# Attention on one core: 64-row products moved in among the scores, and a diagonal block between transposes

## What is computed

```python
xn = layernorm(inputs)                       # gamma, beta
q, k, v = xh @ Wq + bq, xh @ Wk + bk, xh @ Wv + bv     # per head
content = einsum('bqhd,bkhd->bhqk', q + u_bias, k)
pos_score = _rel_shift(einsum('bqhd,khd->bhqk', q + v_bias, p))
attn = softmax((content + pos_score) / sqrt(e))
ctx = einsum('bhqk,bkhd->bqhd', attn, v)
x = layernorm(x + ctx @ Wo + bo)
```

## Time and profile before

| | us |
|---|---|
| median of 3 runs (lowest, highest) | 553.13 (547.18, 553.98) |
| the profiled execution | 551.84 |
| its span, first to last instruction | 550.0 |
| TensorE busy | 452.6 |
| VectorE busy | 356.1 |
| ScalarE busy | 267.4 |
| GpSimd busy | 249.2 |

### The profile page before, as it was taken

The page is one execution under the profiler, slowest core; times in us unless marked ns, Lnnn a source line. Parts: engine busy times, 40 slices in busy tenths (PEclk is TensorE's granted clock), DMA queues, the critical chain, the costliest instruction groups (busy, mean ns, idle before and its releaser), DMA issues. The chain is left out here.

```text
span 550.0 us, 9872 instructions
## 1 busy us (share of the span) xinstructions
PE 452.6 (82%) x3109; PEld 317.3 (58%) x3109; DVE 356.1 (65%) x893; ACT 267.4 (49%) x547; POOL 249.2 (45%) x260
## 2 busy tenths in 40 slices
PE   8798999999999999999857799738979798428870
PEld 7565666656656566666434799613454466327760
DVE  4976676676876777667434466367486566638882
ACT  2356567666666565777401355517546222025653
POOL 3452563446572862440033154442445466425771
PEclk9999999999999999999886899958989978659995
DMA  8499999999999000000040230090000000013405
GB/s 308 109 174 172 170 195 345 189 190 186 194 181 159 3 1 7 16 2 1 2 143 19 63 89 28 13 378 34 0 2 1 1 21 15 24 46 77 103 19 154
DMA packets 69395, 52.72 MB, mean 96 GB/s; under 512 B 3238, under 2 KB 67245, under 8 KB 68704
## 3 DMA queue, kind: packets, MB, share of 16 engines
q1 hardware_dynamic: 66656, 47.84, 44.0%
q0 software_dynamic: 2688, 4.25, 2.6%
HBM read 21.30 MB, written 32.09 MB: 97 GB/s over the span
## 5 line engine op out<-in xcount | busy, mean ns | idle before, releaser
L708 ACT ACTIVATE arena<-banks 128x512 f32<-128x512 f32 x128 | 76.4, 597 | 86.3 <-PE banks L921 86.1
L921 PE MATMUL banks<-ca,work 128*128 128x128 f32 x512 | 82.2, 283 | 18.2 <-ACT arena L708 14.3
L701 ACT ACTIVATE work<-banks,nmax 128x512 f32<-128x512 f32 x128 | 80.7, 686 | 13.7 <-DVE nmax L1321 13.5
L921 PEld LDWEIGHTS banks<-ca,work 128*128 128x128 f32 x512 | 53.6, 140 | 55.5 <-issue 43.0
L1321 DVE TENSOR_REDUCE nmax<-banks 128x2 f32<-128x1024 f32 x64 | 78.3, 1224 | 2.2
L903 PE MATMUL banks<-arena 32*128 32x512 f32 (+3 forms) x256 | 60.1, 435 | 0.0
L892 PEld LDWEIGHTS banks<-arena 32*128 32x128 f32 x256 | 41.2, 184 | 30.4 <-issue 23.2
L892 PE MATMUL banks<-arena 32*128 32x128 f32 x256 | 55.2, 295 | 0.6 <-DVE corr L1401 0.6
L1309 DVE COPY_PREDICATED banks<-ca,banks 128x256 f32<-128x256 uint32 x64 | 27.2, 426 | 38.1 <-PE banks L892 37.9
L1046 PE MATMUL banks<-t,arena 128*128 128x128 f32 x300 | 47.1, 295 | 3.9 <-ACT t L815 1.0
L1101 PE MATMUL banks<-arena 128*128 128x512 f32 x96 | 45.4, 623 | 1.2 <-POOL arena L680 1.2
(11 more groups left out here) (221 smaller groups left out, 828.9 us busy)
## 6 DMA issues: line engine op xcount, KB each, us to landing
regions<-zeros SPq DMA_DIRECT2D x15, 1040.0 KB, 18.4
regions<-zeros SPq DMA_DIRECT2D x9, 1032.0 KB, 19.9
arena<-wp_in SPq DMA_DIRECT2D x1, 4624.0 KB, 26.3
arena<-wp_in SPq DMA_DIRECT2D x1, 4494.0 KB, 15.9
arena<-ct_in SPq DMA_DIRECT2D x2, 1024.0 KB, 9.7
arena<-regions SPq DMA_DIRECT2D x29, 65.0 KB, 1.9
arena<-cb_in SPq DMA_DIRECT2D x1, 1660.0 KB, 8.2
arena<-regions SPq DMA_DIRECT2D x23, 64.5 KB, 1.9
```

Of the source, the lines that this page charges most:

```text
L701: eng.activation(prob[:, r, :], bank[r], ACT.Exp, bias=nmax[:, s % 2, jj:jj + 1]).then_inc(s_exp, 1)
L708: eng.activation(probT[:, v % 2, j0 + jj, :, i % 2 * P:(i % 2 + 1) * P], PT.rearrange("p (t q) -> p t q", t=TB), ACT.Copy).then_inc(s_pTs, 1)
L921: mm = eng.transpose(PT[:, t * P:(t + 1) * P], prob[:, 2 * (s % 2) + jj, t * P:(t + 1) * P], ident)
```

## The change

The products k, t1 and t2 of each group (but for the eleven early jobs) run over the 64 rows of their group alone and are issued inside the scores of a step whose heads lie on the other 64 rows, behind before(1). Such a job is called a rider. The list holds its eviction behind the scores of that step. diagonal(0) of step s+2 is issued between the values and turn(s, 1) of step s. Other jobs move in the plan to make the parities fit.

```diff
+    def ride(step, *events):
+        assert events[0][-1] == (step + 1) % 2
+        behind.setdefault(step, []).extend(events)
...
-    at(0, ("job", "v", 0))
-    at(1, ("job", "k", 0, 1), ("kb", 0, 1))
-    at(2, ("job", "t1", 0, 1))
-    at(3, ("job", "t2", 0, 1), ("q", 0, 1), ("xbo", 0))
+    ride(0, ("job", "k", 0, 1), ("kb", 0, 1))
+    at(1, ("job", "v", 0))
+    ride(2, ("job", "t1", 0, 1))
+    at(3, ("xbo", 0))
+    ride(4, ("job", "t2", 0, 1), ("q", 0, 1))
...
-        first = 3 if b == 1 else 0
+        first = 4 if b == 1 else 0
+        mid = 2 if b == 1 else 0
         at(base if b == 1 else base - 1, ("stats", b))
         at(base + first, ("normz", b))
         at(base + first + 1, ("job", "zT", b))
-        at(base + first + 2, ("job", "k", b, 0), ("kb", b, 0))
-        at(base + first + 3, ("job", "k", b, 1), ("kb", b, 1))
-        at(base + 7, ("job", "t1", b, 0))
-        at(base + 8, ("job", "t2", b, 0), ("q", b, 0))
-        at(base + 9, ("job", "corr", b))
-        at(base + 10, ("job", "t1", b, 1))
-        at(base + 11, ("job", "t2", b, 1), ("q", b, 1))
-        at(base + 13, ("job", "v", b), ("xbo", b))
+        ride(base + first + 2, ("job", "k", b, 1), ("kb", b, 1))
+        ride(base + first + 3, ("job", "k", b, 0), ("kb", b, 0))
+        ride(base + mid + 7, ("job", "t1", b, 0))
+        at(base + mid + 8, ("job", "corr", b))
+        ride(base + mid + 9, ("job", "t2", b, 0), ("q", b, 0))
+        ride(base + mid + 10, ("job", "t1", b, 1))
+        at(base + mid + 11, ("job", "v", b), ("xbo", b))
+        ride(base + mid + 12, ("job", "t2", b, 1), ("q", b, 1))
...
-        at(base + 12, ("job", "ctxT", 2 * b))
+        at(base + (13 if b else 15), ("job", "ctxT", 2 * b))
...
+        if s + 2 < STEPS:
+            plan.append(("diag", s + 2))
         if s < STEPS:
             plan.append(("turn", s, 1))
...
         if s + 2 < STEPS:
             plan.append(("score", s + 2))
+            for e in behind.pop(s, []):
+                put(e)
+                if e[0] == "job":
+                    riders[s + 2] = len(jobs) - 1
...
+            def product(k):
+                name, b, g = jobs[k]
+                rows, part = slice(g * P // NG, (g + 1) * P // NG), queries(name)
+                eng.wait_ge(*after("zT", b))
+                if name == "k":
+                    eng.wait_ge(s_ca[1], 16)
+                    weights = A(f"wk{g}", rows)
+                else:
+                    eng.wait_ge(*after("fold", 0))
+                    n = 2 * g + (name[1] == "2")
+                    weights = wt[rows, n * P:(n + 1) * P]
+                return eng.matmul(job_bank[k][:, part], weights, xnT[rows, part], start=True, stop=True)
+
+            def bank_free(k):
+                at_bank = next(n for n in range(8) if bank[n] is (early[jobs[k][0]] if k < n_early else JOB))
+                if at_bank in used:
+                    eng.wait_ge(*done[used[at_bank]])
+                used[at_bank] = k
...
-                    diagonal(0).then_inc(s_d0, 1)
                     before(1)
+                    if s in riders:
+                        bank_free(riders[s])
+                        product(riders[s]).then_inc(s_job, 1)
                     before(0)
                     behind(1)
                     behind(0)
                     eng.wait_ge(s_d0, s + 1)
-                    diagonal(1).then_inc(s_score, 1)
+                    diagonal(s, 1).then_inc(s_score, 1)
```

More of the change, by code:

```diff
@@ L90, in plan_attention @@
     per = NG * 2 * TB
-    later = {}
+    later, behind, riders = {}, {}, {}
     def at(step, *events):
         later.setdefault(step, []).extend(events)
+    def ride(step, *events):
+        assert events[0][-1] == (step + 1) % 2
+        behind.setdefault(step, []).extend(events)
     for e in (("stats", 0), ("cols", 0), ("kd", 0), ("job", "pem", 0), ("job", "wqT", 0), ("normz", 0), ("job", "bias", 0),
@@ L138, in plan_attention @@
         at(base + 33, ("scatter", b))
-    plan += [("score", 0), ("exp", 0, 0), ("exp", 0, 1), ("qr", 0), ("ids", 0), ("score", 1)]
+    plan += [("diag", 0), ("score", 0), ("exp", 0, 0), ("exp", 0, 1), ("qr", 0), ("ids", 0), ("diag", 1), ("score", 1)]
     for s in range(STEPS + 2 * per + 2):
@@ L154, in plan_attention @@
             plan.append(("score", s + 2))
-    assert not later, later
-    return jobs, plan
+            for e in behind.pop(s, []):
+                put(e)
+                if e[0] == "job":
+                    riders[s + 2] = len(jobs) - 1
+    assert not later and not behind, (later, behind)
+    return jobs, plan, riders
 def plan_recurrence():
@@ L176, in build @@
 def build(nc, x_in, ca_in, ct_in, cb_in, wp0_in, wp1_in, out):
-    jobs, plan = plan_attention()
+    jobs, plan, riders = plan_attention()
     number = {j: k for k, j in enumerate(jobs)}
@@ L868, in ranks, with diagonal @@
                 return mm
-            used = {}
-            for kind, *w in plan:
-                if kind == "score":
+            def diagonal(s, jj):
+                b, g, _, i, j0 = place_of_step(s)
+                rows, mine = slice(HP * (j0 + jj), HP * (j0 + jj + 1)), slice(i * P, (i + 1) * P)
+                return eng.matmul(DA[:, jj * P:(jj + 1) * P], qa[rows, b % 2, g, mine], ka[rows, b % 2, g, mine],
+                                  start=True, stop=True)
+            used = {}
+            def product(k):
[15 more added lines that the diff above has]
+                used[at_bank] = k
+            for kind, *w in plan:
+                if kind == "diag":
+                    s = w[0]
+                    b, g, _, i, j0 = place_of_step(s)
+                    if s:
+                        eng.wait_ge(s_diag, s)
+                    if i == 0 and j0 == 0:
+                        eng.wait_ge(*(s_q, NG * (b - 1) + g + 1) if b else (s_q0, 1 + 2 * g))
+                        eng.wait_ge(s_kb, NG * b + g + 1)
+                    if s == 2:
+                        eng.wait_ge(s_q0, 2)
+                    diagonal(s, 0).then_inc(s_d0, 1)
+                elif kind == "score":
                     s = w[0]
@@ L880, in _ @@
                             eng.wait_ge(*after(name, 0, 0))
[L881 to L887, removed]
                     mine, split = slice(i * P, (i + 1) * P), i * P
[L890 to L893, removed]
                     def before(jj):
@@ L939, in _ @@
                     mm.then_inc(s_pv, 1)
-                elif kind == "job":
+                elif kind == "job" and w[0] not in riders.values():
                     k = w[0]
@@ L943, in _ @@
                     bk = job_bank[k]
[L944 to L948, removed]
+                    bank_free(k)
                     if name == "pem":
@@ L973, in _ @@
                             mm = eng.transpose(bk[:, t * P:(t + 1) * P], z[:, t, :], ident)
[L974 to L977, removed]
                     elif name == "v":
@@ L983, in _ @@
                                             start=True, stop=True)
[L984 to L990, removed]
+                    elif name == "k" or name[0] == "t":
+                        mm = product(k)
                     elif name == "corr":
```

## The result

The change makes the kernel slower: 692.9 us in the median (672.2 to 713.8, 6 runs) against 551.1 (547.2 to 554.0, 6 runs). The forecast was 575, and neither it nor the range to 604 holds the time. Ratios here are of the executions of a kernel that are not set apart as slow and low in clock (for the changed kernel those of 672.2 and 681.7: ratio 1.2285, 95% interval 1.2144 to 1.2426), while the times are medians of all (692.9 against 551.1 is 26% more), since the clock turns out to be part of the effect.

The account below looks back on a forecast made before the run. Plain attention steps were taken as bound by transposes, copy, transposes, copy, exponential (3.33 us). Terms (a) to (g) summed to +22.6 us on 551.84, giving 574.4, plus 1.3 for the median: 575; range 566 to 604.

Parts of the forecast that it names:

- (b): 21 products, as riders inside the scores, run beside the strips on free rows at no cost: 21 x 0.81 = -17.0 us.
- rival B: A 64-row product can't share TensorE with 32-row strips: riders cost 1.06 to 1.69 each, +26.6 us, time 602; chance 0.26.
- (c): The next job waits for the bank until the rider is evicted after VectorE's maximum: 13 x 1.38 = +17.9 us.
- (a): The diagonal moved between values and second transposes delays transposes, copies and exponential: 39 steps x 0.17 = +6.6 us.
- (d): A rider behind a rider, in six steps, waits inside the scores: steps of 4.44 and 4.23 for 3.33, +5.6 us.
- (e): Batch 0's queries on VectorE, which made step 4's merge late, fall in step 5, which waits anyway: -1.2 us.
- (f): In step 17, zT waits for z, queued behind queries and deviations on GpSimd: +3.1 us once.
- (g): Eviction of t1 waits for GpSimd's group 0 queries, delaying v in steps 13, 27, 43: +2.55 each, +7.6 us.
- C: The scores shorten with the first diagonal block taken out: time 561, no measurable change; chance 0.06.
- D: The bank is free in time, so (c), (d) and (g) vanish: time 548, not slower; chance 0.03.

Follow-up runs that it names:

- 64-row run: The changed kernel with dummy 128-row products in TensorE's waits for a rider's eviction and ahead of v and zT; 609.6 us, ratio 1.1072.
- filled kernel with 32-row riders: The changed kernel with riders multiplying only 32 of their 64 rows, and dummy products in TensorE's waits; 575.3 us, ratio 1.0467.

## Why the prediction was wrong

Two of its steps failed, and one was missing.

**(b), that riders are hidden.** It chose the rule on rows over the rule on shape, with 0.62 to 0.26. The trace of before couldn't tell them apart, as it said, and the reason given for the choice (every change of shape there was on shared rows) was no evidence for it. Measured, a 64-row rider costs 0.99, 1.20 and 1.61 more than a hidden one with zero, one and three blocks before the diagonal; rival B had 1.06, 1.26 and 1.69. The 32-row rider costs nothing. Over the whole kernel the step from 32 rows to 64 is worth 609.6 - 575.3 = 34 us, some of it clock (steps 4, 5 and 29 of the 64-row run are at half clock in part); B had 27. What the prediction took from the Trainium skill ("TensorEngine Tiling (Array Packing)", Tiling Modes, Key Properties), that changing the tiling mode drains the engine, agrees with this case (no pass of the scores between 58.44 and 59.49), also for tiles on disjoint rows.

**The clock, in no step.** All prices were taken at full clock, as the earlier trace rows grants it. Nothing asked what happens if it falls. Filled, the same kernel takes 609.6; unfilled 692.9: 83 us, the greatest single term. This is the step that took the time out of the range, since B alone lay within it. The prediction did list 19 waits of a microsecond and more on an engine that had waited 0.2 at a time, and it priced each as its own length only.

**The missing wait.** The diagonal of step 2 now waits in step 0 for VectorE: steps 0 and 1 take 15.8 in place of 10.0 in the filled kernel with 32-row riders, +5.8, where the sum had +0.6 ((c) once, one product less). TensorE's idle time there is 1.11, and most of the rest is half clock. It starts with step 0's first transposes at 19.7 us, ahead of this wait, and lasts until 33; with the diagonal moved from step 4 on only, it is over by 24.

The rest held, where steps at full clock show it:
- (a) a plain step of 3.49 against 3.50; with the diagonal from step 4 on the two shorter executions are at 557 and 560, with +10 by the 0.17 of all 58 steps.
- (c) at full clock steps 5, 10 and 36 take 4.99, 5.38 and 4.99; the sum had 5.10, 5.45 and 5.10 (ctxT or zT 3.72, corr 4.07, and 1.38).
- (d) with 32-row riders, not filled, step 7 takes 4.37 and step 12 4.11; forecast 4.44 and 4.23.
- (e) step 4 no longer has its late merge.
- (f) step 17 takes 6.86 at full clock, in the filled kernel with 32-row riders; forecast 6.8. (The changed kernel's own 7.05 is near it by luck: zT starts at +4.04, earlier than the forecast +4.75, and half clock behind it adds the rest.)
- (g) v at +5.71; forecast +5.7.
- The sum: from step 0's to step 63's first copy, the kernel with hidden riders and filled waits takes 27.5 more than the one before. Without what steps 0 and 1 have over the sum (5.2), and 1.6 for two fillings (steps 4 and 9) where nothing waited, that is 20.7, against 22.6. Its 575.3 matches the forecast partly by luck: the missing wait and the fillings make up for terms that were some 2 us too dear.
- A reading of the earlier trace rows was off without harm: TensorE is at nine tenths from the fifth to the nineteenth slice, not to the twenty-first.

Rivals C and D were wrong: in step 6 the scores still take 1.34 from their first pass to their last one's end (59.49 to 60.83; 1.35 in the earlier trace rows), and TensorE did wait for the evictions. "The prediction is wrong if TensorE waits for no eviction" was the wrong alarm; the row to watch was the granted clock.

So of the 142 us, roughly: 26 for the plan, waits and diagonal (575.3 against 549.5), 34 for the 64-row shape, and 83 for the clock. That the clock's fall hangs on the waits and on the moved diagonal together is shown by three pairs: filling the waits (-83), evicting first (-92), the diagonal back (-68). Each alone takes back about half of the loss or more, and each saves some time of its own besides the clock's, so their shares can't be added. Why the clock stays low for tens of us with TensorE at work, and falls once with no gap ahead, is open.

## What to carry to other kernels

A wait on TensorE costs its own length only while the clock holds; before adding any, ask what clock the engine would have behind it, and try a run with dummy products in the wait. The 64x128 products here did not overlap with 32x128 ones on other rows, and 32x128 ones did, so give what is to run beside a strip the strip's shape. A job that shares one bank should be evicted before the long work in the queue of the engine that evicts it, not behind it.

## What the runs showed of the hardware

- TensorE without a gap in the profile for 82 and 76 us at half clock. The Trainium skill ("TensorE: Matmul & The Clock Gate", Part 1) says that activity releases the throttle. Here both stretches stayed at the lower level with a busy share of 100%, so the busy share in a profile does not tell that the clock will come back.
- An idle wait of 2.00 us, after 37 us at full clock and with the diagonal in its old place, was followed by a mean clock of 0.57 over 6 us; and 44 us at half clock came once with no gap in the 14 us ahead.
- The same idle of 3.1 to 3.2 us was followed by 3.5 us at half clock in one step structure and by 24 in another, one profiled execution each; they differ by one small product between two others of other shapes.
- A 64x128 tile and 32x128 tiles on the other rows: 1.05 us from the product's start to the next pass, 0.86 of them streaming. 32x128 tiles on three strips at once: no cost.
